# Sigmoids and SiLUs of a four-layer attention stack made from tanh, with their products on VectorE

## The reference

```
s1 = jax.nn.silu(conv2d(x, sa_w1, sa_b1, 0))
s2 = jax.nn.silu(conv2d(s1, sa_w2, sa_b2, 1))
spatial_weights = jax.nn.sigmoid(conv2d(s2, sa_w3, sa_b3, 0))
...
fused = jax.nn.silu(combined @ ff_w1.T + ff_b1) @ ff_w2.T + ff_b2
```

## Time and profile before

| what | value |
|---|---|
| median of 3 executions | 5533.32 us (5531.68 to 5542.09) |
| the profiled execution, its own time | 5545.02 us |
| its span, first to last instruction | 5543.2 us |
| mean granted TensorE clock | 0.933 of full speed |
| busy: PE, DVE, ACT, POOL | 91%, 51%, 50%, 58% |
| DMA, HBM | 40 GB/s moved, 12 GB/s of it HBM |

### The profile page before, as it was taken

One profiled execution on the slowest core, in us unless ns is written; L12 is line 12 of the kernel. 1 busy time (PEld: TensorE's weight loads), 2 busy tenths in 40 slices (PEclk: granted clock), 3 DMA queues, 4 the chain that ended last, 5 costly groups with the idle time before them and its releaser, 6 DMA issues.

```text
span 5543.2 us, 63206 instructions
## 1 busy us (share of the span) xinstructions
PE 5032.5 (91%) x22016; PEld 2259.8 (41%) x22016; DVE 2851.5 (51%) x5110; ACT 2752.0 (50%) x4738; POOL 3232.3 (58%) x1777
## 2 busy tenths in 40 slices
PE   7788989999899998999999999999999999899887
PEld 3235333543335433354334543345333453334534
DVE  5345656256553565535655366544566346563362
ACT  3353665345663456524565255652556525555252
POOL 4474667546674476735767357664576636666363
PEclk8899889999899998999989999999899999899999
DMA  2112111022110211102210112101122012120020
GB/s 83 29 29 58 45 45 37 20 58 53 38 30 27 63 48 31 33 21 63 54 40 19 36 49 54 46 12 40 45 54 51 8 44 55 40 52 7 17 49 12
DMA packets 103609, 221.20 MB, mean 40 GB/s; under 512 B 31105, under 2 KB 33409, under 8 KB 103169
## 3 DMA queue, kind: packets, MB, share of 16 engines
q1 hardware_dynamic: 103296, 217.16, 15.1%
HBM read 56.47 MB, written 8.39 MB: 12 GB/s over the span
## 4 chain that ended last, share of the span: by engine, by line
PE 63%; DVE 9%; issue 9%; ACT 9%; POOL 8%; SPq 1%; DMA 1%; POOLq 0%; ACTq 0%; DVEq 0%
PE bank L502 63%; DVE max_cols L943 6%; POOL probs_added L1133 4%; ACT probs L836 3%; POOL probs_added L1120 3%; ACT L836 1%; ACT act L846 1%; DVE dev_squared L1054 1%; DVE stats L1040 1%; ACT act L855 1%; DVE sums_turned L965 1%; SPq L1220 0%; ACT L877 0%; SPq L1209 0%; DVE sums_turned L973 0%
## 5 line engine op out<-in xcount | busy, mean ns | idle before, releaser
L943 DVE TENSOR_REDUCE max_cols<-bank 128x1 f32<-128x512 f32 x3456 | 2183.8, 681 | 1822.3 <-PE bank L502 1818.5
L836 ACT ACTIVATE probs<-bank 128x512 f32<-128x512 f32 x3456 | 1921.2, 599 | 2267.2 <-PE bank L502 2131.4
L1133 POOL TENSOR_TENSOR probs_added<-probs_added,probs 128x1024 f32<-128x1024 f32 x768 | 1801.2, 2369 | 196.4 <-ACT probs L836 195.8
L502 PE MATMUL bank<-q_stack,k_stack 97*128 97x512 f32 (+1 forms) x3584 | 1669.6, 523 | 129.5 <-DVE max_cols L943 66.2
L502 PE MATMUL bank<-probs,v_tokens 128*32 128x512 f32 (+1 forms) x7168 | 1400.0, 649 | 44.1 <-ACT probs L836 44.1
L502 PEld LDWEIGHTS bank<-q_stack,k_stack 97*128 97x128 f32 (+1 forms) x3584 | 666.4, 197 | 891.5 <-issue 461.3
L502 PE MATMUL bank<-act,weight_stream 128*128 128x512 f32 x1792 | 952.8, 632 | 34.2 <-issue 8.3
L1133 POOL TENSOR_TENSOR probs_added<-probs 128x1024 f32<-128x1024 f32 x192 | 452.6, 2369 | 708.8 <-PE bank L502 682.1
L1120 POOL TENSOR_TENSOR probs_added<-probs 128x512 f32<-128x512 f32 x48 | 60.9, 1269 | 883.8 <-PE bank L502 851.9
L502 PE MATMUL bank<-high_parts 32*128 32x512 f32 x3072 | 409.6, 521 | 144.0 <-ACT probs L836 73.6
L502 PEld LDWEIGHTS bank<-probs,v_tokens 128*32 128x32 f32 (+1 forms) x7168 | 329.8, 123 | 515.2 <-issue 362.1
(11 more groups left out here) (82 smaller groups left out, 3479.5 us busy)
## 6 DMA issues: line engine op xcount, KB each, us to landing
k_stack<-high_parts SPq DMA_DIRECT2D x384, 128.0 KB, 2.4
q_stack<-high_parts SPq DMA_DIRECT2D x768, 64.0 KB, 2.0
weight_stream<-stream_dram SPq DMA_DIRECT2D x32, 768.0 KB, 4.4
k_stack<-low_parts SPq DMA_DIRECT2D x192, 128.0 KB, 2.4
q_stack<-low_parts SPq DMA_DIRECT2D x384, 64.0 KB, 2.0
act<-x_dram SPq DMA_DIRECT2D x8, 1024.0 KB, 6.5
act<-pos_dram SPq DMA_DIRECT2D x8, 1024.0 KB, 6.0
weight_stream<-stream_dram SPq DMA_DIRECT2D x16, 512.0 KB, 3.7
```

The source lines that it names most:

```text
L502: return nc.tensor.matmul(dst, lhsT, rhs, start=start, stop=stop, **kw)
L836: act.activation(PR[:, m % P_RING, j, :], bank[:, :], ACT.Exp, scale=att.scale).then_inc(reading(key), 1)
L943: dve.tensor_reduce(cols[:, kh, j, qt:qt + 1], bank[:, :], AX.X, ALU.max).then_inc(reading(key), 1)
L1133: pool.tensor_tensor(ADD[:, js, :], one, two, ALU.add).then_inc(p_added, 1)
```

## The change

SiLU and sigmoid are written with tanh: silu(x) = x (1 + tanh(x/2)) / 2 and sigmoid(x) = (1 + tanh(x/2)) / 2. The factors 1/2 go into constants: the weights of sa2 and sa3, the folded ff weights, and the score scale of the wide heads, whose queries are now twice as large. Halved biases lie in a new tile `halved_bias`, made once at the start.

- sa1 and sa2: ScalarE writes tanh(x/2 + b/2) and x + b (Tanh, then Identity) into a scratch buffer, over 96 rows at once in sa1. VectorE makes (tanh + 1) * (x + b): in sa1 three scalar_tensor_tensor of 32 rows into the padded image, in sa2 one. A semaphore `mixed` takes the place of the bank's read semaphore for PE.
- sa3: ScalarE writes tanh, VectorE adds 1, GpSimd multiplies as before.
- ff1: ScalarE writes tanh into the buffer; VectorE makes (bank + b) * tanh and then (bank + b) + that, both reading the bank, which is given back a little later ("ff1 mix", 0.9 units behind "ff1 out").
- Positions: sa2 starts at 51 and 54 (was 50.5 and 53.5), sa3's first tile at 60.5 (was 60), spatial at 65, 66, 67, 68 (was 63.8 to 68.3 in steps of 1.5). The products' events on VectorE ("mix") are new, at 46.5 and 48.5 (sa1), 55.5 and 58.5 (sa2), 63 and 64.5 (sa3).

The diff, cut to its core:

```diff
-        self.scale = 1.0 / float(np.sqrt({"m": P, "3": C}.get(kind, D)))
+        self.scale = 1.0 / float(np.sqrt({"m": 4 * P, "3": C}.get(kind, D)))
...
-            each("stats", [("a",) + q for q in QUARTERS], 40, 1) + tile("sa1", 0, 2, 43) + tile("sa1", 1, 2, 45) + \
-            norm("norm", 44.5, 3.5, "a", "o") + tile("sa2", 0, 3, 50.5) + tile("sa2", 1, 3, 53.5) + \
-            tile("sa3", 0, 1, 60) + tile("sa3", 1, 1, 62) + each("spatial", QUARTERS, 63.8, 1.5)
+            each("stats", [("a",) + q for q in QUARTERS], 40, 1) + tile("sa1", 0, 2, 43) + curve("sa1", 0, 46.5) + tile("sa1", 1, 2, 45) + curve("sa1", 1, 48.5) + \
+            norm("norm", 44.5, 3.5, "a", "o") + tile("sa2", 0, 3, 51) + curve("sa2", 0, 55.5) + tile("sa2", 1, 3, 54) + curve("sa2", 1, 58.5) + \
+            tile("sa3", 0, 1, 60.5) + curve("sa3", 0, 63) + tile("sa3", 1, 1, 62) + curve("sa3", 1, 64.5) + each("spatial", QUARTERS, 65, 1.0)
...
-            out += tile("ff1", (nh, m), 4, 2.1 + 5 * n, 1.2)
+            out += tile("ff1", (nh, m), 4, 2.1 + 5 * n, 1.2) + curve("ff1", (nh, m), 2.1 + 5 * n + 6)
...
-                        until_read(pe, ("sa1", it.sample, 1))
+                        pe.wait_ge(mixed, MIXED[it.sample, "sa1", 1])
...
-                elif event.endswith(" out"):
+                elif event.endswith(" out") and event != "ff1 out":
...
+                elif event == "ff1 mix":
+                    give(("ff1", it.sample, i))
...
-                elif event == "sa1 out":
-                    if i == 0:
-                        act.wait_ge(border, it.sample + 1)
-                    key = ("sa1", it.sample, i)
+                elif event in ("sa1 out", "sa2 out"):
+                    key = (event[:3], it.sample, i)
...
-                    rows = SIDE // NH
-                    for j in range(3):
-                        ins = act.activation(
-                            padded_image(it.turn)[D * j:D * j + D, 1 + rows * i:1 + rows * (i + 1), 2 - j:2 - j + SIDE],
-                            bank[D * j:D * j + D, :].rearrange("p (r c) -> p r c", c=SIDE), ACT.Silu,
-                            bias=wcol("bsa1", 0, D, D * j))
-                    ins.then_inc(reading(key), 1)
-                elif event == "sa2 out":
-                    key = ("sa2", it.sample, i)
-                    bank = until_full(act, key)
-                    act.activation(act_buf(it.turn, "f")[0:D, 0, half(i)], bank[0:D, :], ACT.Silu,
-                                   bias=wcol("bsa2", 0, D)).then_inc(reading(key), 1)
+                    rows, b = (3 * D, 0) if event == "sa1 out" else (D, 1)
+                    f = act_buf(it.turn, "f")
+                    act.activation(f[0:rows, 1, half(i)], bank[0:rows, :], ACT.Tanh, bias=HALVED[0:rows, b:b + 1],
+                                   scale=0.5).then_inc(curved, 1)
+                    act.activation(f[0:rows, 0, half(i)], bank[0:rows, :], ACT.Identity,
+                                   bias=wcol("b" + event[:3], 0, rows)).then_inc(reading(key), 1)
...
-                    act.activation(act_buf(it.turn, "f")[:, 1, half(i)], bank[:, :], ACT.Sigmoid,
-                                   bias=wcol("bsa3", 0)).then_inc(reading(key), 1)
+                    act.activation(act_buf(it.turn, "f")[:, 1, half(i)], bank[:, :], ACT.Tanh,
+                                   bias=HALVED[:, 2:3], scale=0.5).then_inc(reading(key), 1)
...
-                    key = ("ff1", it.sample, i)
-                    bank = until_full(act, key)
-                    act.activation(act_buf(it.turn, "f")[:, m, half(nh)], bank[:, :], ACT.Silu,
-                                   bias=wcol("bff1", m)).then_inc(reading(key), 1)
+                    bank = until_full(act, ("ff1", it.sample, i))
+                    act.activation(act_buf(it.turn, "f")[:, m, half(nh)], bank[:, :], ACT.Tanh,
+                                   bias=HALVED[:, 3 + m:4 + m], scale=0.5).then_inc(curved, 1)
...
-            for i, dst in enumerate((FF, WV3)):
+            for i, (dst, factor) in enumerate(((FF, 0.5), (WV3, 1.0))):
...
-                dve.tensor_copy(dst[:, :], bank[:, :]).then_inc(reading(("fold", i)), 1)
+                dve.tensor_scalar(dst[:, :], bank[:, :], factor, None, ALU.mult).then_inc(reading(("fold", i)), 1)
+            a, _ = AT["sa2"]
+            mark("halved", dve.tensor_scalar(W[:, a:a + 224], W[:, a:a + 224], 0.5, None, ALU.mult))
+            a, _ = AT["bsa1"]
+            mark("halved", dve.tensor_scalar(HALVED[:, :], W[:, a:a + 5], 0.5, None, ALU.mult))
+            after("halved")
...
+                elif event == "sa1 mix":
+                    if i == 0:
+                        dve.wait_ge(border, it.sample + 1)
+                    until_read(dve, ("sa1", it.sample, i))
+                    rows, f = SIDE // NH, act_buf(it.turn, "f")
+                    for j in range(3):
+                        r = slice(D * j, D * j + D)
+                        u, v = (f[r, k, half(i)].rearrange("p (r c) -> p r c", c=SIDE) for k in (1, 0))
+                        ins = dve.scalar_tensor_tensor(
+                            out=padded_image(it.turn)[r, 1 + rows * i:1 + rows * (i + 1), 2 - j:2 - j + SIDE],
+                            in0=u, scalar=1.0, in1=v, op0=ALU.add, op1=ALU.mult)
+                    ins.then_inc(mixed, 1)
+                elif event == "sa2 mix":
+                    until_read(dve, ("sa2", it.sample, i))
+                    u, v = (act_buf(it.turn, "f")[0:D, k, half(i)] for k in (1, 0))
+                    dve.scalar_tensor_tensor(out=v, in0=u, scalar=1.0, in1=v, op0=ALU.add, op1=ALU.mult)\
+                       .then_inc(mixed, 1)
+                elif event == "sa3 mix":
+                    until_read(dve, ("sa3", it.sample, i))
+                    u = act_buf(it.turn, "f")[:, 1, half(i)]
+                    dve.tensor_scalar(u, u, 1.0, None, ALU.add).then_inc(mixed, 1)
+                elif event == "ff1 mix":
+                    nh, m = i
+                    dve.wait_ge(curved, CURVED[it.sample, i])
+                    key = ("ff1", it.sample, i)
+                    bank, f = PS[tiles[key][0]], act_buf(it.turn, "f")[:, m, half(nh)]
+                    mark("curve", dve.scalar_tensor_tensor(out=f, in0=bank[:, :], scalar=wcol("bff1", m), in1=f,
+                                                           op0=ALU.add, op1=ALU.mult))
+                    after("curve")
+                    dve.scalar_tensor_tensor(out=f, in0=bank[:, :], scalar=wcol("bff1", m), in1=f, op0=ALU.add,
+                                             op1=ALU.add).then_inc(reading(key), 1)
...
-                    until_read(pool, ("sa3", it.sample, nh))
+                    pool.wait_ge(mixed, MIXED[it.sample, "sa3", nh])
```

More of the change, by code:

```diff
@@ L274 @@
 PLAN = list(plan())
-SCALED, RAISED, COLOURED = {}, {}, {}
+SCALED, RAISED, COLOURED, MIXED, CURVED = {}, {}, {}, {}, {}
+_curves = 0
 for _name, _it, _i in PLAN:
@@ L283 @@
         COLOURED[_it.sample, _i] = len(COLOURED) + 1
+    elif _name in ("sa1 out", "sa2 out", "ff1 out"):
+        _curves += 1
+        if _name == "ff1 out":
+            CURVED[_it.sample, _i] = _curves
+    elif _name in ("sa1 mix", "sa2 mix", "sa3 mix"):
+        MIXED[_it.sample, _name[:3], _i] = len(MIXED) + 1
 def first_quad(s):
@@ L769, in _ @@
                     nh, _ = i
-                    until_read(pe, ("sa2", it.sample, nh))
+                    pe.wait_ge(mixed, MIXED[it.sample, "sa2", nh])
                     product(("sa3", it.sample, nh), 1, 0, slice(0, P),
```

4 lines of the change are left out of this document (added).

## The result

The changed kernel took **5463.96 us** in the median of its runs (5453.81 to 5468.66); the kernel before, run beside it on the same chip, 5537.7 us. The ratio is 0.9861 with a 95% interval of 0.9842 to 0.988, so it is faster by 74 us, 1.4%. The forecast was 5466 us with a range of 5375 to 5530. One of the four executions of a later experiment, the version with all biases that reads PSUM, took 6184.09 us at a mean granted clock of 0.73, and its median and ratio are those of the other three.

What follows compares the result with a forecast made beforehand. TensorE was taken as busy 91% of the span, with ScalarE's table loads counting only where PE waits, mainly in the gate. -42 - 25 = -67 us took the profiled 5545.0 to 5478, as median 5466 us; range 5375 to 5530.

Steps and rivals of the forecast that it cites:

- third piece of the gate: u56 to u68: six loads a turn go from ScalarE, the bound there; 6.0 us a turn, 42 us in 7 turns.
- first piece: u42 to u50: VectorE's products hold back the maxima for u50, so no gain; bounds 4.5 us gained, 9.5 lost a turn.
- second piece: u50 to u56 of the gate: PE stays busy at the low clock, PEclk near 0.56; no gain.
- ff1: u1 to u26: PE's idle time behind exps and lost clock go, less delayed maxima; 3.6 us a turn, 25 us in all.
- everything else: Turn 0's gate, turn 8's ff1 and the halvings at the start: zero, within 3 us.
- rival C: Loads were covered: third piece stays at 18.2 us, ff1's delay moves to maxima; 17 us gained, 5516 us; chance 0.13.
- each product lets one addition past: sa1 in the gate: each VectorE product waits for one GpSimd addition, so three take 3 x (0.75 + 2.37) = 9.4 us.
- Rival A: Clock comes back in u50 to u56: 8 us a turn plus 4.5 from u42 to u50, 87 us, 5379 us; chance 0.25.
- sa2 and sa3: Gate: four single VectorE operations, 0.75 to 3.1 us a turn, hidden by its idle time; uncovered, 9.5 us a turn.
- the 1.5 us taken off for delayed maxima: ff1: VectorE's products delay maxima by 1.5 us four times a turn; one counted, 5.1 - 1.5 = 3.6 us.
- B: VectorE's queue, u46 to u66, becomes the wait: 9.5 us a turn, 66 us slower, 5599 us; chance 0.12.
- T1: Theory set up after the result: loads cost PE's waits behind ScalarE; products with two SBUF operands, waiting for GpSimd, return part.

Runs made afterwards that it cites:

- the version with all biases that reads PSUM: Changed kernel with ScalarE adding 1 to tanh and VectorE making one product, (bank + bias) x (1 + tanh), for sa1, sa2 and ff1: 5447.96 us, ratio 0.983.
- the next experiments: The block of 2.06 us: changed kernel with sa1 and sa2 products reading the PSUM bank, Identities and their bias left out; 5441.71 us, ratio 0.9834.
- the first two versions that read PSUM: Changed kernel with sa1 and sa2 products reading PSUM, without Identities and their bias (5441.71 us), and the variant keeping all biases, ScalarE adding the 1 (5447.96 us).
- the last experiment: Changed kernel with both groups of three sa1 products moved behind the maxima, from 46.5 and 48.5 to 49.1 and 49.2: 5497.47 us, ratio 0.9929.
- The three versions whose products read PSUM: Changed kernel with products reading PSUM: bias left out (5441.71 us), all biases kept (5447.96 us), and the latter with sa1's products on units of their own (5449.35 us).

## Why the prediction was right, and where it was not

The medians moved by 74 us where 67 were forecast, and the spans of the profiled executions by 83. Term by term, over the seven turns:

| term | forecast | measured |
|---|---|---|
| third piece of the gate | 42 us | 26.2 us |
| first piece | 0 | 15.4 us |
| second piece | 0 | -2.3 us |
| ff1 | 25 us | 37.7 us |
| everything else | 0 | 6.0 us |

So the way and the two places were right, and that 5466 lies 2 us from 5463.96 is luck. In the gate, 16 us too many in the third piece and 15 too few in the first cancel. The sum was 16 us short of the profiled difference. Against that, the profile of before lay 7 to 12 us above its medians and that of after 2 below its own, which is worth 9 us, and the median of before was 5537.7 us beside the changed kernel, 4 more than the 5533.3 from which the forecast was counted.

**Loads in the third piece** (forecast 20.65 to 14.7 us, 42 us in all). Right in the four turns like turn 2, which took 14.19 us at full clock. The 14.7 us stood between PE's 13 at full clock and its 15.3 at 0.83 and were not worked out from more; the mean over the seven turns is 16.8. As the working had it, ScalarE was the bound there and PE is next (13.06 us busy, ScalarE 11.48). What it missed is that PE's time there is 13 us only if the clock is back. In turns 1 and 7 it is not, PE is busy for 22.4 us, and the piece is 2 us longer than before, which was the prediction's own sign of rival C (above 18 us) for these two. This is the mis-sized term of the gate. The bounds (2.5 to 8.6 us gained a turn) left this out: the worst case was taken as PE's 18.2 us of before, in which the clock was low for only a part.

**First piece** (forecast 0). It gained 2.2 us a turn. The step that failed is that each product lets one addition past, so that three take 9.4 us, and under it that "the additions follow each other without a gap": the first three took 4.76 us, because GpSimd had run out of exps for 0.59 us when the second began, and the second three 2.79 us. A block of 4.76 us is nearly as long as the 4.63 it replaced, and PE's stall of 3.58 us returned as one of 3.70; that the block sets the stall fits the next experiments, where a block of 2.06 us left one of 1.22. Of the 2.2 us gained, 1.07 lie in the shorter gap ahead of it: the 1.41 us behind an exp are 0.34 now. The rest isn't traced to a wait. The experiment with products that read PSUM shows the mechanism as forecast (two SBUF operands wait for GpSimd, one does not); only how often it strikes was wrong. The page's rule on the shared port (the Trainium skill, Advanced Engine Details and Errata, VectorE Performance Modes) holds here both ways, also in that GpSimd's addition stretches, from 2.36 to 2.85 us. That L1115 never waited in 16 times (680 ns at most) is no exception: none of the 16 began beside an addition.

**Second piece** (forecast: low clock, no gain). Right: 18.31 us at 0.58, against 18.17 at 0.56. Rival A, that the clock would come back, did happen in the experiment that only removes the loads, in turns 1, 2 and 7. There PE's stall at u50 is 1.57 us, 2.1 shorter than in the changed kernel. That the shorter stall brought the clock back isn't shown: behind the same stall the second piece was at 0.51 to 0.68 in the four other turns of that kernel, and the first two versions that read PSUM have stalls of 1.2 to 1.7 us there and ran the second piece at 0.50 to 0.56 in every turn.

**sa2 and sa3** (forecast: hidden). Right for PE. sa3's "+1" does wait, up to 1476 ns, and GpSimd's gate multiplication waited for it for 77.9 us in all, but no stall of PE between u42 and u68 of turn 2 ends with it. At its shortest it takes 415 ns, against 679 for a maximum. That agrees with the page VectorE: DVE Perf Modes (Mode 2x_2P) of the Trainium skill, by which it was estimated at about half of a maximum (it is 0.61). It was also blocked: eight of the 16 began beside a GpSimd multiplication, took 761 to 1476 ns and ended 0.28 us after its end, and the other eight took 415 to 426 ns.

**ff1** (forecast 25 us). It gave 37.7. This is the mis-sized term outside the gate. The 5.1 us for PE's idle time and the clock were near (5.6 measured in turns with the clock at 0.96 before, 3.97 in turn 3), but the 1.5 us taken off for delayed maxima did not come: PE's idle time behind maxima in the stretch is 0.43 and 0.27 us, as before. The eight products took 0.73 to 0.75 us each, as the nearest row said, and all of it lies in VectorE's idle time (busy 23.1 of 35.1 us). Even the bound of 5.1 us a turn was low, against 5.4 in the mean.

**Rivals B and C.** B, a slower kernel through waits on VectorE, did not come, but the last experiment shows that it was near: with the same instructions started 0.7 to 2.6 units later, 33 of the 74 us are lost. C fell with ff1 and with the third piece of five turns.

**What stays open.** What decides how long the clock stays low. Turns 1 and 2 of the changed kernel have first pieces alike to 0.01 us (14.78 and 14.79) and 0.5 and 0.58 in the second, 0.54 and 1.00 in the third. The clock's fall comes at a different place in the stall (11.6 us after u42 in turn 1, 13.2 in turn 2), and no experiment here controls that place. Of T1 the experiments show what the loads were worth and that products with two SBUF operands wait; its rival is right in that far shorter stalls than those of before are also followed by the low clock. The three versions whose products read PSUM save 15 to 17 us more than the changed kernel, each against its own run of before, and the kernel in which only the loads were removed saves 44 more. So the wait for GpSimd explains at most some 16 of the 44 us, since those versions drop other instructions as well; that the clock holds most of the rest is likely and not shown.

## What to carry to other kernels

Price a table load by the engine that waits behind it, stretch by stretch: here 186 us of ScalarE were worth 118 us, and in the profiled pair of executions (161 us apart) 100 us lay in the gate and 38 in ff1. In the gate the loads held back the exps that PE waited for, and a stretch of low clock followed. When an activation is taken apart into products on VectorE, let each product read one factor from PSUM if GpSimd adds beside it; a product with two SBUF factors that begins beside a GpSimd instruction waits for its end, and whoever queues behind it waits too. And where TensorE's clock is on an edge, give the estimate both outcomes for every stretch behind a stall: a stall of 1.57 us was followed by 11.1 us in one turn and by 19.7 in another. A total that comes out right can still hide this: here the terms were off by 16, 15 and 13 us, and partly cancelled.

## What the runs showed of the hardware that was not expected

- In the changed kernel a VectorE product with both factors in SBUF waited only if a GpSimd addition was under way when it began: it then ended 0.54 to 0.55 us after that addition's end (21 times, 1.27 to 2.74 us), and took 0.67 to 0.68 us otherwise (43 times). An addition that began just behind such a product took 2.85 us in place of 2.36.
- One factor in PSUM removes the wait wholly: 666 to 686 ns in 48 times, and 729 to 749 ns in 48 times with the bias added, some 40 of them begun beside an addition in each.
- A tensor_scalar of 128x512 from SBUF to SBUF took 415 to 426 ns alone and 761 to 1476 ns where it began beside a GpSimd multiplication.
- Stretches with the same instructions and stalls alike to some hundredths of a microsecond ran 57.7 and 47.3 us in one execution, and 38.5 and 47.5 in another kernel, with TensorE's granted clock as the difference (0.54 and 1.00 in the third piece of the first pair, 1.00 and 0.51 in the second piece of the other).
